# A three-stage transformer layer: prologue joined with cross-attention, grouped attention's end joined with feed-forward

## The chip, the core and the metric

The kernel runs on one core of a Trainium2 chip. The metric is the device time of one execution, in microseconds (us). Engines are named as in the profile: PE (TensorE, matrix products), PEld (its weight loads), DVE (VectorE), ACT (ScalarE), POOL (GpSimd), SP (SyncE, which here only issues DMAs). ACT can issue DMAs too.

## The reference, cut to what matters

```
x   = x + xattn(layernorm(x), ctx)          # x: 8 x 64 x 512, ctx: 8 x 1601 x 512
x   = x + attn(layernorm(x), cache)         # 32 heads, 8 key heads, 16 blocks of 32 cached keys + 64 new ones
x   = x + ffn(layernorm(x))                 # 512 -> 1792 -> 512
xattn: q = (xn @ Wq_d @ W_qk) as 16 heads of 32;  c = ctx @ Wkv_d (1601 x 32)
       out = softmax(q @ c.T / sqrt(32)) @ (c @ Wv_u)
ffn:   W = base + mean(|w - base|) * sign(w - base);  out = (silu(x @ W1.T) * (x @ W3.T)) @ W2.T
```

All in float32. A product that needs the accuracy is made as three products of a high and a low part ("high" a rounded copy, "low" the difference).

## The kernel before, in words

x has 512 tokens: four tiles of 128 rows. Each stage is a block in which every engine has its own program; semaphores order them, and at a block's end all engines meet. There are six blocks.

1. **load_and_constants**: SP loads x (one DMA of 1 MB), the small weights and the contexts of batches 0 and 1 (3.2 MB each). DVE and ACT make the layer norm of all four tiles at once (`normalise`, `root`), PE turns them (L157), ACT copies them out. POOL makes the identity, masks and zeros.
2. **cross_queries**: PE makes the 64 latent query features (L341) and then, head by head, 16 products (L349); for each ACT takes the high part (L358) and DVE the low part (L366) into `q_t`.
3. **cross_attention**: for each batch, `compress` (L580, L584) makes the 32 latent features c of 1601 keys from the context; ACT copies them (L752) and rounds them (L757); POOL makes the low part (L550); SP places them with 15 DMAs (`place_keys`, L497, L499) in the stacked key tile `c_t` (rows: high, low, high). `max_scores` (L618; 16 per batch) with `take_max` on DVE (L813) finds the row maxima, `turn_max` and `shift_row` (L626, L761) put them in `q_t`; then `scores` (L639), exponentials on ACT (L745), values and denominators on PE, pair sums on POOL (L536, L543). Batch b+1's maxima run inside batch b. Beside this, a side job sums |w - base| of the feed-forward weights in 8 slices: SP loads three pieces, POOL subtracts (L529), ACT sums (L766); slice 0 before batch 0, slice b+1 in batch b. The 32 DMAs that gather the selected cache blocks (L293, L296) are the last thing on SP's queue, in batch 6.
4. **rotated_keys**: layer norm 2 and the keys and values of grouped attention.
5. **grouped_attention**: 32 heads in a software pipeline, `head(g, i, this, last, nxt)`: the scores of this head (L1089), turning of the last head's probabilities (L1104, L1105), its mix with the values (L1113 to L1122), queries of the next. After each group of four heads, `output` (L1137) makes the output projection of all four tiles, and DVE adds it to x (L1310). The last head's probabilities are handled by `head(NKV, 0, False, True, False)`, followed by `output` of the last group.
6. **feed_forward**: the three means (L1485, L1428, L1488), layer norm 3, and 14 chunks of 128 hidden features. A chunk's weights are prepared by POOL (difference, L1401), ACT (sign, L1443), DVE (`prepare`: quantise, L1477), ACT (high, L1449) and DVE (low, L1482), two chunks ahead of PE's `gates` (24 products of 512 columns, L1411) and `down` (12 products, L1421).

## Time and profile before

| | |
|---|---|
| three runs, median (lowest, highest) | 978.36 us (976.01, 979.28) |
| the profiled execution's own time | 976.39 us |
| its span, first to last instruction | 974.6 us |
| PE busy | 900.9 us (92%) |
| DVE, ACT, POOL busy | 618.2, 508.8, 402.8 us |
| mean granted TensorE clock | 0.964 of full |

A row of the trace's timeline is: start, duration, engine, line, operation, output<-inputs, shapes, count, and in brackets the idle time of the engine before it with what ended it. Rows with a count are merged.

### The profile page before, as it was taken

Reading aid. Unit: us, or ns where it says so; the run is one execution under the profiler, and the core shown is the slowest. Engines: PE = TensorE matmul, PEld = TensorE weight load, DVE = VectorE, ACT = ScalarE, POOL = GpSimd, SP = SyncE. Lnnn points to the kernel's source line nnn. Section 1 sums busy time; section 2 is a strip of 40 time slices with the busy share of each in tenths; the row PEclk is TensorE's granted clock in tenths of the full one; section 3 lists DMA queues with packets and bytes.
Section 4 is the critical chain, followed back from the end, with each engine's and each line's share of the span. In section 5 each row is a group of like instructions: output and inputs, shape, how many; then the busy total and the mean of one; then the engine's idle time right before and its main releaser. Section 6 shows DMA issues by size and latency. Waiting matters only on the chain. (4 is left out here: it accounts for less than half of the span.)

```text
span 974.6 us, 15256 instructions
## 1 busy us (share of the span) xinstructions
PE 900.9 (92%) x5298; PEld 653.6 (67%) x5298; DVE 618.2 (63%) x994; ACT 508.8 (52%) x995; POOL 402.8 (41%) x264
## 2 busy tenths in 40 slices
PE   4868999999998879999999999999999997599997
PEld 2334455545453658888888888888888886488886
DVE  3453567656671538767577675757757575688883
ACT  2315666666665546636365463645636364355551
POOL 3025778777876024323234232333323231344430
PEclk9857999999999889999999999999999999799999
DMA  9374765642440721111010110101101000465521
GB/s 331 128 257 185 276 258 210 241 157 96 153 143 2 259 76 44 45 33 49 20 51 22 43 43 22 43 22 43 43 22 43 12 1 1 153 206 201 194 90 43
DMA packets 46178, 103.70 MB, mean 106 GB/s; under 512 B 11314, under 2 KB 16434, under 8 KB 45106
## 3 DMA queue, kind: packets, MB, share of 16 engines
q1 hardware_dynamic: 44754, 102.94, 30.8%
q8 instruction: 29, 0.48, 0.2%
q10 hardware_dynamic: 1376, 0.13, 0.2%
q14 instruction: 19, 0.16, 0.0%
HBM read 97.08 MB, written 1.05 MB: 101 GB/s over the span
## 5 line engine op out<-in xcount | busy, mean ns | idle before, releaser
L1336 POOL TENSOR_TENSOR head_probs<-head_probs,inverse_den 128x576 f32<-128x576 f32 x128 | 147.0, 1148 | 298.3 <-DVE inverse_den L1267 298.2
L813 DVE TENSOR_REDUCE max_part<-psum 128x1 f32<-128x804 f32 x128 | 120.9, 989 | 57.7 <-PE psum L618 57.7
L745 ACT ACTIVATE probs<-psum 128x512 f32<-128x512 f32 (+1 forms) x208 | 107.9, 601 | 51.8 <-PE psum L639 47.4
L1214 ACT ACTIVATE head_probs<-psum,neg_max 128x576 f32<-128x576 f32 x128 | 94.6, 739 | 76.6 <-PE psum L1105 43.0
L536 POOL TENSOR_TENSOR prob_sums<-probs 128x1024 f32<-128x1024 f32 x48 | 114.4, 2389 | 26.2 <-PE psum L669 14.0
L1280 DVE TENSOR_REDUCE neg_max<-psum 128x1 f32<-128x576 f32 x128 | 96.1, 754 | 36.2 <-PE psum L1089 28.2
L1260 DVE TENSOR_TENSOR probs_t_low<-psum,probs_t_high 128x512 fp32r<-128x512 f32 x128 | 87.5, 684 | 9.0 <-ACT probs_t_high L1220 7.9
L618 PE MATMUL psum<-c_t,q_t 96*128 96x402 f32 x256 | 80.2, 402 | 11.7 <-DMA c_t<-c_high 7.3
L1089 PE MATMUL psum<-k_high,query_t_high 128*128 (+1 forms) x256 | 84.1, 329 | 5.0 <-DVE query_t_low L1245 2.9
L618 PEld LDWEIGHTS psum<-c_t,q_t 96*128 96x128 f32 x256 | 47.0, 206 | 58.0 <-DVE max_part L813 30.7
L1104 PE MATMUL psum<-ident,head_probs 128*128 128x128 f32 x512 | 78.3, 275 | 5.7 <-DVE mixed_t_low L1305 3.9
L639 PE MATMUL psum<-q_t,c_t 97*128 97x512 f32 (+1 forms) x208 | 73.1, 430 | 6.6 <-ACT probs L745 5.1
L1220 ACT ACTIVATE probs_t_high<-psum 128x512 fp32r<-128x512 f32 x128 | 75.1, 587 | 2.7 <-PE psum L1105 2.7
L1104 PEld LDWEIGHTS psum<-ident,head_probs 128*128 128x128 f32 x512 | 58.0, 140 | 27.4 <-issue 22.1
L1089 PE MATMUL psum<-k_low,query_t_high 128*128 (+1 forms) x256 | 75.5, 295 | 0.0
L1089 PE MATMUL psum<-k_high,query_t_low 128*128 (+1 forms) x256 | 75.3, 294 | 0.0
L1401 POOL TENSOR_TENSOR ffn_quant<-ffn_raw 128x1536 f32<-128x1536 f32 x14 | 49.0, 3500 | 56.4 <-DVE ffn_w_low L1482 52.5
L1310 DVE TENSOR_TENSOR x<-psum,x 128x512 f32<-128x512 f32 x32 | 22.1, 692 | 59.9 <-PE psum L1137 59.9
L652 PE MATMUL psum<-probs,c_nat 128*32 128x512 f32 (+1 forms) x416 | 59.5, 605 | 0.0
L1228 ACT ACTIVATE wo_t_high<-wo_nat 128x512 fp32r<-128x512 f32 x32 | 20.2, 631 | 72.4 <-PE psum L1137 72.4
L529 POOL TENSOR_TENSOR w_raw<-w_raw 128x896 f32<-128x896 f32 x24 | 50.5, 2106 | 16.8 <-DMA w_raw<-in_L_ffn_mean_w_dram 16.8
L639 PEld LDWEIGHTS psum<-q_t,c_t 97*128 97x128 f32 (+1 forms) x208 | 37.9, 189 | 28.7 <-ACT probs L745 21.3
(160 smaller groups left out, 1914.4 us busy)
## 6 DMA issues: line engine op xcount, KB each, us to landing
cache<-in_ctx_dram SPq DMA_DIRECT2D x4, 3202.0 KB, 11.5
ctx_t_odd<-in_ctx_dram SPq DMA_DIRECT2D x4, 3202.0 KB, 11.4
w_raw<-in_L_ffn_w_dram SPq DMA_DIRECT2D x24, 448.0 KB, 5.1
w_raw<-in_L_ffn_mean_w_dram SPq DMA_DIRECT2D x24, 448.0 KB, 6.1
ffn_raw<-in_L_ffn_w_dram SPq DMA_DIRECT2D x42, 256.0 KB, 3.8
ffn_raw<-in_L_ffn_mean_w_dram SPq DMA_DIRECT2D x42, 256.0 KB, 4.1
wq_nat<-in_L_attn_wq_dram SPq DMA_DIRECT2D x32, 256.0 KB, 2.7
wo_nat<-in_L_attn_wo_dram SPq DMA_DIRECT2D x32, 256.0 KB, 2.6
```

Of the source, the lines that this page charges most:

```text
L536: pool.tensor_tensor(sums[u][:, :], prob_buffer(b, 2 * u)[:, :], prob_buffer(b, 2 * u + 1)[:, :], ALU.add).then_inc(s_add, 1)
L618: mm = pe.matmul(psum[:, bank + k, 0:PIECE_KEYS], q_t[0:SHIFT, b, 2 * qt:2 * qt + 2, :].rearrange("p h n -> p (h n)"), c_t[0:SHIFT, b % 3, ...
L639: pe.matmul(psum[0:rows_of(t), n % SCORE_BANKS, :], lhs, rhs[:, half * BANK:(half + 1) * BANK], start=True, stop=True).then_inc(s_sb, 1)
L745: act.activation(prob_buffer(b, t)[0:rows, half * BANK:(half + 1) * BANK], psum[0:rows, n % SCORE_BANKS, :], ACT.Exp, scale=XSCALE).then_i ...
L813: dve.tensor_reduce(max_part[:, qt, pair:pair + 1], psum[:, bank:bank + 2, 0:PIECE_KEYS], AX.XY, ALU.max).then_inc(s_max, 1)
L1089: mm = pe.matmul(psum[:, bank, 0:HALF], q_t[a][:, qt * P:(qt + 1) * P], (k_high, k_low)[b][:, keys], start=(step == 0), stop=(step == 2))
L1104: pe.transpose(bank[:, t * P:(t + 1) * P], probs[:, qt, t * P:(t + 1) * P], core.ident[:, :])
L1214: act.activation(probs[:, qt, :].rearrange("p (a k) -> p a k", a=2), psum[:, 2 * (qt % 2):2 * (qt % 2) + 2, 0:HALF], ACT.Exp, bias=neg_max ...
L1220: act.activation(probs_t[0][:, 0:ST, qt * P:(qt + 1) * P], psum[:, turn_bank(qt), :].rearrange("p (t q) -> p t q", t=ST), ACT.Copy).then_i ...
L1260: dve.tensor_tensor(probs_t[1][:, 0:ST, qt * P:(qt + 1) * P], psum[:, turn_bank(qt), :].rearrange("p (t q) -> p t q", t=ST), probs_t[0][:, ...
L1280: dve.tensor_reduce(neg_max[:, qt:qt + 1], psum[:, 2 * (qt % 2):2 * (qt % 2) + 2, 0:HALF], AX.XY, ALU.max, negate=True).then_inc(s["max"], 1)
L1336: pool.tensor_tensor(probs[:, qt, :], probs[:, qt, :], rden[:, qt:qt + 1].to_broadcast([P, KEYS]), ALU.mult).then_inc(s["norm"], 1)
```

## The change

The first three blocks become one, `cross_attention`, and the last two become one, `attention_and_ffn`.

- **Queries by tile of x.** x is loaded as four DMAs, context 0 as four. Tile 0 is normalised, turned and made into queries at once (`latent_queries(0)`, `queries(0)`), which serves batches 0 and 1. Tiles 1 to 3 come after `compress(0)`: turning, `latent_queries(1)`, and `queries(1)` to `queries(3)` between batch 0's maxima, after the 5th, 8th and 11th. A `queries(j)` is 8 products of 128 columns for head pairs. For tiles 1 to 3 ACT takes the high part of each (two instructions, `queries_high`) and a plain copy (two, `queries_copied`, into the probability buffers, which are still free), and POOL subtracts (two). `scores(0, 0)` waits for all four tiles' low parts.
- **Keys placed from two queues.** For batch 0, SP issues the high and the low rows, ACT the second high rows. For the later batches SP issues high, high, low.
- **The side job** runs one batch later: slice b in batch b, slice 7 in batch 7, its loads behind the cache gather on SP's queue.
- **Early constants.** The three means are made at the start of grouped attention; the exp table is loaded on ACT before batch 0's keys are rounded.
- **Grouped attention's end by tile.** Chunk 0's weights are prepared during the last group of heads (`early_weights`), chunk 1's in the last mix. Feed-forward buffers lie over dead ones (`over`). The last head's turned tiles go to banks 4, 5, 2, 3 and its tail to bank 7 instead of 6. The output projection of the last group is issued in parts, and layer norm 3 runs tile by tile behind them: DVE makes the moments and an offset, ACT the scaled tile (`tile_offset`, `tile_scale`), PE turns it between output parts. The gate products of chunks 0 and 1 are made first for tiles 0 and 1, then for tiles 2 and 3, with 256 columns each.

```diff
+QUERIES_AT = {4: 1, 7: 2, 10: 3}
...
+            pe.wait_ge(s_mask, 1)
+            norm.tile_turn(pe, 0)
+            latent_queries(0)
+            queries(0)
+            pe.wait_ge(s_wkv, 16)
+            compress(0)
+            natural(0)
+            for j in range(1, TT):
+                norm.tile_turn(pe, j)
+            latent_queries(1)
             for i in range(MAXIMA):
                 max_scores(0, i)
+                if i == 1:
+                    compress(1)
+                if i == 3:
+                    natural(1)
+                if i in QUERIES_AT:
+                    queries(QUERIES_AT[i])
             turn_max(0)
+            pe.wait_ge(s_qhi, 2 * TT)
+            pe.wait_ge(s_qlo[1], 2 * (TT - 1))
+            pe.wait_ge(s_wv, 32)
             scores(0, 0)
...
@@ scalar, before batch 0
+            compressed_high(0)
+            act.wait_ge(s_chi, 1)
+            place_part(act, 0, 2 * LKV, c_high)
+            norm.rest_root(act)
...
+            for j in range(1, TT):
+                queries_high(j)
+                queries_copied(j)
...
@@ sync, after place_keys(7)
-            load_pieces(BATCH - 1, 1)
-            load_pieces(BATCH - 1, 2)
+            load_pieces(BATCH - 2, 1)
+            load_pieces(BATCH - 2, 2)
             sp.wait_ge(s_idx, 16)
             gather_cache(core, sp, index)
+            for i in range(3):
+                load_pieces(BATCH - 1, i)
...
@@ tensor, grouped attention: after queries of head 0
+            pe.wait_ge(s_tot, 1)
+            pe.matmul(psum[:, 6, 0:3], ones[:, :], total[:, :], start=True, stop=True).then_inc(s_all, 1)
+            pe.wait_ge(s_co, 1)
             run(pe, head)
+            for qt in range(TT):
+                turn_last(qt)
+            pe.wait_ge(s["wol"], REP * NKV)
+            output_part(0, range(0, 2))
+            mix(NH - 1)
+            output_part(0, range(2, 3))
+            output_part(1, range(0, 3))
+            output_part(0, range(3, 4))
+            output_part(1, range(3, 4))
+            output_part(2, range(REP))
+            norm.tile_turn(pe, 0)
+            output_part(3, range(0, 2))
+            norm.tile_turn(pe, 1)
+            output_part(3, range(2, REP))
+            pe.wait_ge(norm.s_low, TT // 2)
+            gate_products(0, 0, early)
+            norm.tile_turn(pe, 2)
+            gate_products(0, 1, early)
+            norm.tile_turn(pe, 3)
+            for k in range(2):
+                gate_products(1, k, early)
+            pe.wait_ge(norm.s_low, TT)
+            for c in range(2):
+                for k in range(2):
+                    gate_products(c, k, late).then_inc(s_gu[k], 1)
+            down(0)
```

On PE, from the start of the program to batch 0's scores. Before (L341, L349 are the queries, L580 and L584 compress, L618 the maxima):

```order
L157 MATMUL psum<-ident,norm_normed 128x128 x16
L341 MATMUL psum<-xn_t,wq_d 64x512 x4
L349 MATMUL psum<-cq_t,w_qk 64x512 x16
...
L580 MATMUL psum<-ctx_t_odd,wkv_d 32x384 x16
L584 MATMUL psum<-ctx_t_odd,wkv_d 32x65 x16
...
L618 MATMUL psum<-c_t,q_t 128x402 x32
L626 MATMUL psum<-ident,max_row 97x128 x8
```

Now (L752 and L768 are the queries, L635 and L639 compress, L674 the maxima):

```order
L752 MATMUL psum<-xn_t,wq_d 64x384 x4
L674 MATMUL psum<-c_t,q_t 128x402 x4
L635 MATMUL psum<-ctx_t_odd,wkv_d 32x384 x16
L639 MATMUL psum<-ctx_t_odd,wkv_d 32x65 x16
L674 MATMUL psum<-c_t,q_t 128x402 x4
L647 MATMUL psum<-ident,c_parts 128x128 x3
L648 MATMUL psum<-ident,c_parts 65x32
L674 MATMUL psum<-c_t,q_t 128x402 x2
L768 MATMUL psum<-cq_t,w_qk 128x128 x8
L674 MATMUL psum<-c_t,q_t 128x402 x6
L768 MATMUL psum<-cq_t,w_qk 128x128 x8
```

Batch 1's compress and the queries of tiles 1 to 3 have moved from ahead of batch 0's maxima to between them.

On ACT in the same stretch, now (L884 takes the high parts, L891 the copies):

```order
L856 ACTIVATE c_high<-c_parts 128x449
L469 DMA c_t<-c_high 32x384 x4
L471 DMA c_t<-c_high 32x65
L179 ACTIVATE norm_rstd<-norm_rstd 128x3
L225 ACTIVATE xn_t<-psum 128x4x128 x3
L879 ACTIVATE cq_t<-psum 64x384
L910 ACT_TABLE_LOAD
L910 ACTIVATE exp_table_warm<-ones_by_latent 128x1
L851 ACTIVATE c_parts<-psum 128x449
L856 ACTIVATE c_high<-c_parts 128x449
L884 ACTIVATE q_t<-psum 64x16x64 x2
L891 ACTIVATE probs<-psum 32x1024 x2
```

The root of tiles 1 to 3 (L179) stands behind five DMA issues.

On PE at the seam of attention and feed-forward, now (L1403 is the output projection, L215 the turning of a normalised tile, L1413 the gate products):

```order
L1403 MATMUL psum<-wo_t_high,mixed_t_low 128x512
L215 MATMUL psum<-ident,wq_nat 128x128 x4
L1403 MATMUL psum<-wo_t_high,mixed_t_high 128x512
...
L1403 MATMUL psum<-wo_t_high,mixed_t_low 128x512
L1413 MATMUL psum<-attn_x_high,ffn_w_high_4251 128x256 x4
L1413 MATMUL psum<-attn_x_low,ffn_w_high_4251 128x256 x4
L1413 MATMUL psum<-attn_x_high,ffn_w_low_4252 128x256 x4
L215 MATMUL psum<-ident,wq_nat 128x128 x4
L1413 MATMUL psum<-attn_x_high,ffn_w_high_4251 128x256 x4
```

The turning, which stood in one piece of 16 behind all outputs, now lies between output parts and gate products.

## Rows read from the trace of the kernel before

**Rows 1.** The page, part 1: busy time, share and instructions of each engine.
```profile
PE 900.9 (92%) x5298; PEld 653.6 (67%) x5298; DVE 618.2 (63%) x994; ACT 508.8 (52%) x995; POOL 402.8 (41%) x264
```
**Rows 2.** Timeline of PE, from the start to batch 0's scores.
```profile
43.25 2.79 PE L580 MATMUL psum<-ctx_t_odd,wkv_d 128*32 128x384 f32 x32
...
55.17 1.71 PE L618 MATMUL psum<-c_t,q_t 96*128 96x402 f32 x4 [7.29 <-DMA c_t<-c_high]
...
77.32 1.65 PE L639 MATMUL psum<-q_t,c_t 97*128 97x512 f32 x3 [1.11 <-ACT q_t L761]
```
**Rows 3.** Windows: PE, PEld, DVE, ACT, POOL busy, PEclk, DMA share, GB/s.
```profile
10.00:20.00 10.00, 7.20 (x24) 4.29 (x24) 3.18 (x11) 3.00 (x6) 0.00 (x0) 1.00 0.96 412
...
60.00:70.00 10.00, 8.92 (x19) 4.77 (x20) 8.85 (x11) 2.20 (x6) 3.14 (x2) 0.50 0.81 240
```
**Rows 4.** Timelines of SP, DVE, ACT and POOL: unit costs used for the start.
```profile
7.14 0.51 SPq L283 DMA_DIRECT2D cache<-in_ctx_dram  x1
...
44.48 2.52 SPq L497 DMA_DIRECT2D c_t<-c_high  x4
...
63.53 1.89 DVE L813 TENSOR_REDUCE max_part<-psum 128x1 f32<-128x804 f32 x2 [0.23 <-PE psum L618]
...
76.25 1.02 ACT L761 ACTIVATE q_t<-psum 1x1024 fp32r<-1x1024 f32 x1 [12.03 <-PE psum L626]
77.28 1.28 ACT L745 ACT_TABLE_LOAD   x1
...
111.07 1.02 ACT L761 ACTIVATE q_t<-psum 1x1024 fp32r<-1x1024 f32 x1 [0.47 <-PE psum L626]
...
141.42 1.02 ACT L761 ACTIVATE q_t<-psum 1x1024 fp32r<-1x1024 f32 x1 [0.47 <-PE psum L626]
...
310.52 2.35 POOL L543 TENSOR_TENSOR prob_sums<-prob_sums,probs 65x1024 f32<-65x1024 f32 x1
```
**Rows 5.** Timelines of SP and POOL in batches 6 and 7: gather, subtractions, sums.
```profile
287.64 0.37 SPq L296 DMA_DIRECT2D cache<-in_L_attn_v_cache_dram  x1
...
272.64 2.11 POOL L529 TENSOR_TENSOR w_raw<-w_raw 128x896 f32<-128x896 f32 x1
...
293.24 2.37 POOL L536 TENSOR_TENSOR prob_sums<-probs 128x1024 f32<-128x1024 f32 x1 [5.09 <-PE psum L669]
```
**Rows 6.** Timelines of PE and DVE at the start of grouped attention.
```profile
356.51 0.40 PE L1089 MATMUL psum<-k_high,query_t_high 128*128 128x288 f32 x1 [1.41 <-DVE query_t_low L1245]
...
356.37 0.68 DVE L1241 TENSOR_TENSOR wq_t_low<-wq_nat,wq_t_high 128x512 fp32r<-128x512 f32 x1
```
**Rows 7.** Timeline of PE at the seam of attention and feed-forward.
```profile
813.73 1.07 PE L1122 MATMUL psum<-probs_t_low,value_high 128*128 128x512 f32 x4
...
816.30 0.63 PE L1104 MATMUL psum<-ident,head_probs 128*128 128x128 f32 x4 [1.50 <-DVE mixed_t_low L1305]
...
821.41 1.19 PE L1113 MATMUL psum<-probs_t_high,value_high 128*128 128x512 f32 x4 [1.53 <-DVE probs_t_high L1291]
...
841.86 3.68 PE L157 MATMUL psum<-ident,norm_normed 128*128 128x128 f32 x16 [4.15 <-DVE norm_normed L146]
...
850.52 2.04 PE L1411 MATMUL psum<-ffn_x_high,ffn_w_high 128*128 128x512 f32 x4 [4.99 <-DVE ffn_w_low L1482]
```
**Rows 8.** The chain that ended last: start, us, what.
```profile
866.34 5.60 PE psum L1411 x24
871.95 2.76 PE psum L1421 x12
```
**Rows 9.** Timelines of DVE and POOL in the feed-forward chunks.
```profile
851.85 5.22 DVE L1477 SCALAR_TENSOR_TENSOR ffn_quant<-ffn_quant,coeff,ffn_raw 128x512 f32<-128x512 f32 x3 [0.27 <-ACT ffn_quant L1443]
...
869.03 2.06 DVE L1500 TENSOR_TENSOR hidden_low<-hidden,hidden_high 128x512 fp32r<-128x512 f32 x1 [0.70 <-ACT hidden_high L1465]
...
867.03 3.50 POOL L1401 TENSOR_TENSOR ffn_quant<-ffn_raw 128x1536 f32<-128x1536 f32 x1 [4.49 <-DVE ffn_w_low L1482]
...
875.02 3.52 POOL L1401 TENSOR_TENSOR ffn_quant<-ffn_raw 128x1536 f32<-128x1536 f32 x1 [4.49 <-DVE ffn_w_low L1482]
```

More of the change, by code:

```diff
@@ new lines, in gate_products @@
+            def gate_products(c, k, cols):
+                pe.wait_ge(s_wl, 3 * c + k + 1)
+                for step, (a, b) in enumerate(PASSES):
+                    for i in range(DC):
+                        mm = pe.matmul(psum[:, gate_bank(c, k), cols], w_t[c % SLOTS][a][:, k, i * P:(i + 1) * P],
+                                       (xh, xl)[b][:, i, cols], start=(step == 0 and i == 0),
+                                       stop=(step == 2 and i == DC - 1))
+                return mm
@@ new lines, in gates, with down @@
+            def gates(c, k):
+                wait(pe, s_silu if k == 0 else s_h, c - 1)
+                gate_products(c, k, slice(0, TOK)).then_inc(s_gu[k], 1)
+            def down(c):
+                pe.wait_ge(s_hl, c + 1)
+                pe.wait_ge(s_wl, 3 * c + 3)
+                for qt in range(TT):
+                    for step, (a, b) in enumerate(PASSES):
+                        mm = pe.matmul(psum[:, qt, :], hid[c % 2][a][:, qt * P:(qt + 1) * P],
+                                       w_t[c % SLOTS][b][:, 2, :], start=(c == 0 and step == 0),
+                                       stop=(c == CH - 1 and step == 2), skip_group_check=True)
+                mm.then_inc(s_d, 1)
@@ new lines, in _ @@
+            for j in range(TT - 1):
+                norm_tile(j)
+            for j in range(2):
+                norm.tile_low(dve, j)
+            norm_tile(TT - 1)
+            for j in range(2, TT):
+                norm.tile_low(dve, j)
+            for c in range(CH):
+                dve.wait_ge(s_silu, c + 1)
+                dve.wait_ge(s_gu[1], c + 1)
+                wait(dve, s_hl, c)
+                dve.tensor_tensor(hidden[:, :], psum[:, gate_bank(c, 1), :], gate[:, :], ALU.mult).then_inc(s_h, 1)
+                dve.wait_ge(s_hh, c + 1)
+                dve.tensor_tensor(hid[c % 2][1], hidden[:, :], hid[c % 2][0], ALU.subtract).then_inc(s_hl, 1)
+                if c + 2 < CH:
+                    for k in range(3):
+                        quantise(c + 2, k)
+                    for k in range(3):
+                        low(c + 2, k)
@@ L1322, in _ @@
+            dve.wait_ge(s_d, CH)
+            for j in range(TT):
+                dve.tensor_tensor(core.x[:, j, :], psum[:, j, :], core.x[:, j, :], ALU.add).then_inc(s_x, 1)
         @block.gpsimd
```

854 lines of the change are left out of this document (499 added, 355 removed).

## The prediction

> **What bounds the kernel now.** I read the page's engine shares first, then PE's timeline, then the timelines of whatever PE waited for. PE is busy 92% of the span [rows 1], so the change can only win in the stretches where PE idles or runs at half clock. There are two long ones, and the change touches both.
>
> The first is the start. Batch 0's maxima begin at 55.17, after PE has waited 7.29 us for the last placed keys, and its scores begin at 77.32 [rows 2]. Between 60 and 70 PE is busy 8.92 of 10 us, but at a granted clock of 0.50, the 1.2 GHz level [rows 3]: it does one pair of score products per reduction of DVE, every 1.06 us (1.89 / 2 plus 0.23 / 2) [rows 4].
>
> The second is the seam. The last full mix ends at 814.80 (813.73 + 1.07), the gate products begin at 850.52 [rows 7], and from there PE runs without a gap at 8.36 us a chunk (5.60 + 2.76) [rows 8].
>
> **The start.** DMA moves 412 GB/s when loaded [rows 3], so a context (1601 x 512 x 4 bytes, 3.28 MB) takes 8.0 us. SP's small loads end at 7.14 [rows 4], and these are unchanged. Context 0 is thus in at about 17 (7.1 + a latency that I put at 2 + 8), tiles 1 to 3 of x (0.8 MB) at 19, context 1 at 27. Tile 0's queries fit in front of that. compress(0) costs only its last quarter behind the last byte, the two copies 1.1, so the high keys are there at 20.5. Placing five DMAs costs 3.1 us of issue (2.52 for four) [rows 4]. SP issues high and low, 20.5 to 26.8, and with 2 us to land the keys are complete at 29. ACT issues the third part until 23.7. Behind it on ACT is the root of tiles 1 to 3, and behind that the normalised tiles (1.5), turning, copies (1.7) and the latent queries (2.7 at full, 5.4 at half clock): 30 to 33. The queue of ACT, not the keys, releases the first maxima; I take **31.5**.
>
> Then PE has eleven maxima ahead of queries(3), 11 x 1.06 = 11.7, with compress(1) 3.4 (2.79 [rows 2] and its tail), natural(1) 0.8 and three query sets between them. A query set does as many passes as a quarter of the old queries, 1.8 us at full clock. That is 9.6 more if nothing overlaps. PE has half of each 1.06 to spare at full clock, but the waits for banks let it use little of that, and I take off 0.8: 31.5 + 11.7 + 8.8 = 52.0. For the last tile ACT then makes four instructions over 1024 columns, 4 x 1.02 = 4.1, and POOL two, 2 x 2.35 = 4.7 (the nearest row has 65 partitions instead of 32; the duration goes by columns, since 128 partitions take 2.37 [rows 4, 5]). No instruction of this shape is in the trace. Scores at 52.0 + 8.8 = **60.8**, against 77.3: **-16.5**. Compress(1), which would have been late before, is covered by the maxima; what is late next is this chain of copies and subtractions, since scores(0, 0) waits for all of it. Bounds: everything at half clock, 70 (-7); full overlap, 56 (-21).
>
> Batch 0 itself takes 34.8 us from shift row to shift row (76.25 to 111.07), batch 1 30.35 [rows 4]. Of the 4.5 in excess 1.28 is the exp table's load, which moves to where ACT waits anyway; the other 3.2 is mostly half clock. PE will still idle for the subtractions before the scores, so I give back half: **-2.9** (bounds -1.3 and -4.5).
>
> **Batch 7.** The side job's last slice is now in the batch that has no maxima beside it. Its loads stand behind the gather, whose last issue is at 287.64; the first sum starts at 293.24 [rows 5]. With six 0.45 MB loads landing from 293 to 297.5, each of the three subtractions (2.11 [rows 5]) is in POOL's way. POOL is idle a little between sums, so not all 6.3 count; following its queue I get the last sum 3.2 later, and the denominators wait for it: **+3.2** (bounds 0 and +6.3). ACT's three extra sums fit in its waits.
>
> **Start of grouped attention.** The means' matmul waits for DVE behind the second query weight (0.68 [rows 6]) and a 0.16 us scaling; the first scores wait with it: **+0.8** (bounds 0 and +1.5). It was hidden nowhere, since PE already waits 1.41 here.
>
> **The seam.** Between 814.80 and 850.52 lie 35.7 us. PE's work in it: turning four tiles of the last head 2.4 (4 x about 0.6), 14 mix products and 48 outputs at 0.23 (2.76 / 12 [rows 8]) 14.3, the turning of x at most 3.7 [rows 7] and 2.9 at full clock, one matmul 0.35: 19.9. So 15.8 is waiting or slow, and the first eight gate products, at half clock (four take 2.04 [rows 7]), lose 0.23 each, 1.8 more. Now no block ends, and chunks 0 and 1 are prepared. What still waits, following the queues: the mix for the last low tile 1.5, the fourth head's low part 0.6 (ACT has chunk 1's signs in front of it), tile 0's turning 1.0 (DVE has three low parts of chunk 1 in front of its sum, then moments, root on ACT, offset, scaling: 3.1 behind the sum), the low parts of tiles 0 and 1 1.6. That is 4.7. Products of 256 columns instead of 512 cost 0.4 more in total. Sum: 15.8 + 1.8 - 4.7 - 0.4 = **-12.5** (bounds -8, if each norm tile costs a microsecond more, and -15). The chunks' preparation in the last group adds some 4 us of work to DVE and 3 to ACT over three heads; they are busy 63% and 52% [rows 1] and wait for PE at each head's end, so I cost it at nothing (1 us on the mix if that cover is gone). Early buffers, banks and the loop removal cost nothing on any queue.
>
> **Sum.** -16.5 - 2.9 + 3.2 + 0.8 - 12.5 = -27.9. Against the profiled execution's own 976.39 that is 948.5; the median of the three runs is 2.0 higher, and I add half of that: **949.5 us**.
>
> **Rivals.**
> 1. *The query chain at half clock.* PE does compress(1) and the queries at 1.2 GHz, as it did the maxima from 60 to 70 at 89% busy [rows 3]. Scores at 70 instead of 60.8: 959. For: the clock was low there before. Against: then PE had no work between the reductions; compress(1) alone is a run of several us. Chance 0.20.
> 2. *Better than forecast.* Maxima and queries overlap fully and batch 0 runs at full clock: 56 and 1.6 less, 943. Against: the waits for banks. Chance 0.13.
> 3. *The seam pays little.* The tile-by-tile norm is a chain DVE, ACT, DVE, ACT, PE, ACT, DVE, and PE finds too little between: a gain of 6 instead of 12.5, 956. For: four such chains share two queues. Against: 15 output products (3.4 us) stand between tile 0's last one and its turning, and 18 for tile 1. Chance 0.10.
> 4. *Slower, by the preparation of chunks.* DVE and POOL make a chunk every 7.99 us (867.03 to 875.02 [rows 9]), PE needs 8.36. That holds because POOL's 3.5 us subtraction falls on one short DVE instruction, which takes 2.06; where it fell on the three of L1477, they took 5.22 [rows 9] instead of 2.06. The chunks now start in another phase. If POOL stays on L1477, the period is 7.99 + 3.2 = 11.2, and 12 chunks lose 2.8 each: +34, 982. The change turns into a loss above a period of 8.36 + 27.9 / 12 = 10.7. Against: POOL's subtraction waits for the low parts of the chunk before, as it did, so it starts at the same place of DVE's program. Chance 0.02.
>
> The Trainium skill, "SBUF — State Buffer", section "Who interferes with whom", says that a DVE instruction with two SBUF inputs and a GpSimd instruction that reads SBUF exclude each other for a whole instruction, and that issue order decides who waits. The 5.22 and the 2.06 above agree; by that rule alone, with the order left open, rival 4 would be as likely as the forecast, and what sets the order here is the semaphore.
>
> 5. *The change does not do what it says*: SP's loads or a shared bank serialise tile 0's early start, and the start ends where it did. Only the seam is left, less batch 7: 968. Chance 0.03.
>
> **Chances.** Forecast 0.52, rivals as above; the cases join at their edges. A measurement of this kernel can tell about 0.3%, 3 us, from no change. Every case but the fourth lies below 975. With 0.01 for a seam and a start that both disappoint further, and 0.01 for a loss that I don't see: faster 0.96, within 0.3% 0.01, slower 0.03. The range goes from 941 (rival 2 with the better seam) to 961 (rival 1 with 1 us of spread on each side); left out are rivals 4 and 5 and the tails.
>
> **What would show it.** First maxima near 31, with PE's wait ended by the tiles' latent queries; POOL's six subtractions one behind the other, the last ending at the first scores, near 61; shift rows of batch 1 near 92. In batch 7 the last sum 3 us later after the first. First gate products some 22 us behind the last full mix instead of 36, and 8.36 a chunk after them. I am wrong if the wait before the scores is on something else than POOL, if PE's gaps at the seam add up to more than 8 us, or if a chunk takes more than 8.4.

## The result, and the profile after the change

| | before | after |
|---|---|---|
| runs side by side, median (lowest, highest) | 977.18 us (974.94, 979.28) | 946.72 us (943.43, 948.39) |
| ratio, 95% interval | | 0.9684, 0.9645 to 0.9724 |
| the profiled execution's own time, its span | 976.39, 974.6 | 948.39, 946.6 |
| mean granted TensorE clock | 0.964 | 0.976 |

The change takes 30.5 us off the median. The forecast was 949.5.

The page's first part, against [rows 1]: PE has 11 us less busy time in 28 us less span. It does more products (half-width gates), and a smaller share of the span is at half clock (granted 0.976 instead of 0.964).

```profile
PE 889.5 (94%) x5386; PEld 658.9 (70%) x5386; DVE 604.5 (64%) x988; ACT 516.9 (55%) x1005; POOL 416.3 (44%) x270
```

**The start.** Timelines of ACT, PE, POOL and PE, against [rows 2]. The columns are start, duration, engine, line, operation, operands, count, and in brackets the wait with what ended it.

```profile
24.19 0.20 ACT L179 ACTIVATE norm_rstd<-norm_rstd 128x3 f32<-128x3 f32 x1 [4.17 <-issue]
...
28.75 5.38 PE L752 MATMUL psum<-xn_t,wq_d 128*64 128x384 f32 x8 [0.69 <-ACT xn_t L225]
...
34.05 1.28 PE L674 MATMUL psum<-c_t,q_t 96*128 96x402 f32 x4
...
47.11 13.93 POOL L603 TENSOR_TENSOR q_t<-probs,q_t 32x1024 fp32r<-32x1024 f32 x6 [6.17 <-ACT probs L891]
...
61.14 2.24 PE L695 MATMUL psum<-q_t,c_t 97*128 97x512 f32 x4 [2.35 <-POOL q_t L603]
```

ACT takes the roots 4.17 us late, behind its own five DMA issues. The latent queries run at half clock (5.38 for 8 products). The maxima start at 34.05 instead of 55.17. POOL's six subtractions stand one behind the other, 2.32 each, and end at 61.04. PE's wait of 2.35 for them is what releases the scores, 16.2 earlier than at 77.32.

**Batch 7.** Timeline of POOL, against [rows 5]. The first subtraction waits 4.81 us for the load behind the gather, and two more stand between the sums. The last sum ends at 300.44, 29.8 behind the shift row (270.62); before, it was 25.3.

```profile
276.03 2.09 POOL L543 TENSOR_TENSOR w_raw<-w_raw 128x896 f32<-128x896 f32 x1 [4.81 <-DMA w_raw<-in_L_ffn_mean_w_dram]
...
298.07 2.37 POOL L557 TENSOR_TENSOR prob_sums<-prob_sums,probs 65x1024 f32<-65x1024 f32 x1
```

**Start of attention.** PE now waits for the coefficients, 1.97 instead of 1.41 [rows 6].

```profile
344.87 0.40 PE L1309 MATMUL psum<-k_high,query_t_high 128*128 128x288 f32 x1 [1.97 <-DVE coeff L1712]
```

**The seam.** Timeline of PE from the last full mix (804.65 = 803.58 + 1.07) to the first gate product, 20.7 us instead of 35.7 [rows 7].

```profile
803.58 1.07 PE L1342 MATMUL psum<-probs_t_low,value_high 128*128 128x512 f32 x4
...
808.79 1.20 PE L1333 MATMUL psum<-probs_t_high,value_high 128*128 128x512 f32 x4 [0.56 <-DVE probs_t_high L1717]
...
819.29 0.66 PE L215 MATMUL psum<-ident,wq_nat 128*128 128x128 f32 x4 [0.22 <-ACT wq_nat L209]
...
821.70 0.66 PE L215 MATMUL psum<-ident,wq_nat 128*128 128x128 f32 x4 [0.38 <-ACT wq_nat L209]
...
825.33 0.74 PE L1413 MATMUL psum<-attn_x_high,ffn_w_high 128*128 128x256 f32 x4 [1.57 <-DVE attn_x_low L230]
```

The waits add up to 2.7 us. The chain that ended last shows where they come from (start, us, what): chunk 1's transfer ends at 806.38, then POOL's subtraction, ACT's signs and DVE's six instructions for the chunk's weights (with one low part of the last mix between them), and only behind these DVE's sum for tile 0 of x. The last line is one tile's turning.

```profile
801.26 5.12 DMA ffn_raw<-in_L_ffn_mean_w_dram
806.38 0.07 issue
806.44 3.50 POOL ffn_quant L1788
809.96 1.50 ACT ffn_quant L1547
811.49 2.08 DVE ffn_quant L1698 x3
813.57 0.60 DVE mixed_t_low L1727
814.16 1.80 DVE ffn_w_low L1703 x3
815.97 0.61 DVE x L1681
...
827.03 0.44 PE psum L215 x4
```

**The chunks.** The chain again, against [rows 8], and POOL and DVE, against [rows 9]:

```profile
848.88 5.44 PE psum L1413 x24
854.32 2.72 PE psum L1427 x12
```
```profile
841.22 3.50 POOL L1788 TENSOR_TENSOR ffn_quant<-ffn_raw 128x1536 f32<-128x1536 f32 x1 [5.56 <-DVE mixed_t_low L1703]
...
843.28 2.00 DVE L1751 TENSOR_TENSOR probs_t_low<-hidden,probs_t_low 128x512 fp32r<-128x512 f32 x1 [0.70 <-ACT probs_t_low L1592]
```

A chunk takes 8.16 us instead of 8.36, which the prediction did not have. POOL's 3.5 us still fall on the one short instruction of DVE, so rival 4 did not come true.

In sum, between the two profiles: start -16.2, batch 0 -0.7, batch 7 +4.5, start of attention +0.8, heads +1.5, last full mix to the gates of chunk 2 -15.5, twelve chunks -2.4: -28.0, the difference of the spans.

### The profile page after: what moved, and what is told of

Its sections match the earlier page's. It is cut to its first block, busy times and chain, and to the rows that moved or that the text cites. A ratio compares the mean times of both kernels' runs of the same rounds, so it can differ in the third digit from the quotient of the medians.

```text
span 946.6 us, 15443 instructions
## 1 busy us (share of the span) xinstructions
PE 889.5 (94%) x5386; PEld 658.9 (70%) x5386; DVE 604.5 (64%) x988; ACT 516.9 (55%) x1005; POOL 416.3 (44%) x270
## 4 chain that ended last, share of the span: by engine, by line
PE 54%; DVE 5%; ACT 2%; issue 2%; POOL 1%; DMA 1%; DVEq 0%; SPq 0%; ACTq 0%
PE psum L1309 9%; PE psum L1413 8%; PE psum L1357 8%; PE psum L1295 7%; PE psum L1324 6%; PE psum L1427 4%; PE psum L1333 3%; PE psum L1338 3%; PE psum L1342 3%; DVE neg_max L1644 1%; PE psum L1325 1%; PE psum L1334 1%; PE psum L1336 1%; DVE probs_t_low L1624 1%; DVE mixed_t_low L1670 1%
## 5 line engine op out<-in xcount | busy, mean ns | idle before, releaser
L1624 DVE TENSOR_TENSOR probs_t_low<-psum,probs_t_high 128x512 fp32r<-128x512 f32 x124 | 84.8, 684 | 6.4 <-ACT probs_t_high L1525 5.4
L1324 PE MATMUL psum<-ident,head_probs 128*128 128x128 f32 x496 | 75.9, 275 | 3.2 <-DVE mixed_t_low L1670 2.4
L674 PE MATMUL psum<-c_t,q_t 96*128 96x402 f32 x256 | 74.4, 375 | 4.7 <-DVE max_part L945 2.9
L674 PEld LDWEIGHTS psum<-c_t,q_t 96*128 96x128 f32 x256 | 44.1, 192 | 48.1 <-DVE max_part L945 26.5
L1788 POOL TENSOR_TENSOR ffn_quant<-ffn_raw 128x1536 f32<-128x1536 f32 x13 | 45.5, 3506 | 68.0 <-DVE ffn_w_low L1703 26.9
L1525 ACT ACTIVATE probs_t_high<-psum 128x512 fp32r<-128x512 f32 x124 | 72.8, 587 | 0.0
L708 PE MATMUL psum<-probs,c_nat 128*32 128x512 f32 (+1 forms) x416 | 60.4, 613 | 0.0
L1309 PEld LDWEIGHTS psum<-k_high,query_t_high 128*128 128x128 f32 x256 | 48.8, 190 | 9.9 <-ACT head_probs L1519 4.6
L1681 DVE TENSOR_TENSOR x<-psum,x 128x512 f32<-128x512 f32 x32 | 22.1, 690 | 52.4 <-PE psum L1357 52.4
```

The lines of the kernel that those rows point to most:

```text
L674: mm = pe.matmul(psum[:, bank + k, 0:PIECE_KEYS], q_t[0:SHIFT, b, 2 * qt:2 * qt + 2, :].rearrange("p h n -> p (h n)"), c_t[0:SHIFT, b % 3, ...
L1309: mm = pe.matmul(psum[:, bank, 0:HALF], q_t[a][:, qt * P:(qt + 1) * P], (k_high, k_low)[b][:, keys], start=(step == 0), stop=(step == 2))
L1324: pe.transpose(bank[:, t * P:(t + 1) * P], probs[:, qt, t * P:(t + 1) * P], core.ident[:, :])
L1624: dve.tensor_tensor(probs_t[1][:, 0:ST, qt * P:(qt + 1) * P], psum[:, turn_bank(qt), :].rearrange("p (t q) -> p t q", t=ST), probs_t[0][:, ...
```

## The experiments

Each time is a median. Times of one group were measured on one chip beside the same runs of the kernel before, and a ratio is to these. The first group: 1 to 4. The second: 5, 7, 8, 9. The third: 6, 10, 11, 12. The unedited changed kernel ran beside the third group only (0.9701); in the others its ratio of 0.9684 (0.9645 to 0.9724), from another chip, has to serve.

**1. The start alone.** The changed prologue and cross-attention, with grouped attention and feed-forward of the kernel before (whole functions exchanged).

> The prologue and cross-attention of the changed kernel, with the grouped attention and the feed-forward of the kernel before. Theory (the two halves of the change are independent): the first scores stand at 61.1 us and batch 7 gives back about 4.5, so the first product of the heads stands 11.6 us before that of the kernel before (at 344.9), and nothing after it moves: the time is 965 us (977 less 12). A chunk of the feed-forward keeps the 8.36 us of the kernel before. Rival A (the shorter chunk of 8.16 us comes from the start, as from where the program's code or buffers lie): 8.16 a chunk here and 962.5. Rival B (the 1.5 us that the heads lost belongs to the start): first head product at 344.9 but the last full mix only 10 us earlier, 967.

963.88 us, ratio 0.9886 (0.9844 to 0.9929). Scores at 60.7. The first head product stands at 339.9, 5 us earlier than forecast, and the last full mix ends at 798.25, since the heads take 458.4 us. But the end, from there on, takes 164.3 instead of 159.8: the granted clock fell to half in the last head's mix too (its four low products take 1.91 us instead of 1.07). A chunk takes 5.60 + 2.76 = 8.36, so rival A falls, and so does rival B, since the heads lose nothing here.

**2. The seam alone.** The prologue and cross-attention of the kernel before with the joined attention and feed-forward.

> The prologue and cross-attention of the kernel before, with the attention and feed-forward in one block of the changed kernel. Theory: the last full mix ends 1 to 1.5 us later than before (a chunk's weights are prepared by VectorE in the last two heads, and TensorE waits for it), from its end to the gates of chunk 2 it takes 35.9 us where it took 51.4, and 12 chunks at 8.16 instead of 8.36 give 2.4: 977 + 1.2 - 15.5 - 2.4 = 960.5. Rival A (the chunk's length belongs to the start): 8.36 a chunk, 963. Rival B (the seam is gained only because the start made room before it): above 966.

957.82 us, ratio 0.9838 (0.9792 to 0.9883). From the last full mix to the end 141.9 us, as in the changed kernel (141.95), and 8.16 a chunk. The heads take 459.5. The theory's 960.5 was 2.7 too high, and both rivals fall. The ratios of experiments 1 and 2 multiply to 0.9726; the whole change has 0.9684, and 0.9701 (0.9670 to 0.9731) in experiment 12. Within these intervals the halves are independent.

**3. The roots first.**

```diff
+            norm.rest_root(act)
             act.wait_ge(s_chi, 1)
             place_part(act, 0, 2 * LKV, c_high)
-            norm.rest_root(act)
```

> The changed kernel with one step moved: ScalarE takes the roots of tiles 1 to 3 ahead of placing its part of the keys, instead of behind it. Theory (ScalarE's five transfers, 4.1 us, hold up the roots, and with them the tiles' turning, the latent queries and the first maxima, and all up to the scores follows one for one): the roots at 21.4 instead of 24.2, first maxima at 31 instead of 34.05, scores at 58.3 instead of 61.1, 944 against 946.7. Rival A (the keys' placing becomes late by the same step: maxima wait for the keys until about 32.5): scores at 59.6, 945.2. Rival B (TensorE, colder, runs the maxima at half clock for longer and gives it back): scores at 61, 946.7.

944.07 us, ratio 0.9692 (0.9659 to 0.9724). That is the changed kernel's own ratio, so the total does not show what the trace does; experiment 4 beside it took 947.64. The root stands at 21.56 instead of 24.19 (2.6 earlier), the latent queries at 27.37 instead of 28.75 (1.4 earlier), since now the copies of the turned tiles wait behind ACT's issues instead. Maxima at 32.2 (1.8 earlier), POOL's first subtraction at 45.0 instead of 47.1, scores at 59.2, nearer to rival A's numbers than to the theory's, but not by the keys: ACT's 4.2 us of issuing were only shifted to its next instructions.

**4. Tile 3's low part on DVE.**

```diff
-            for j in range(1, TT):            # POOL
+            for j in range(1, TT - 1):
...
+            for odd in range(2):              # DVE, behind negate_max(0)
+                dve.tensor_tensor(query_rows(TT - 1, odd, 2 * LKV, SHIFT), query_bank(TT - 1, odd, LKV),
+                                  query_rows(TT - 1, odd, 0, LKV), ALU.subtract).then_inc(s_qlo[1], 1)
```

> The changed kernel with the low part of query tile 3 taken by VectorE straight from PSUM behind batch 0's maxima (2 x 1.25 us), instead of by ScalarE's copy (2.0 us) and GpSimd (2 x 2.32 us). Theory (GpSimd's six subtractions bound the scores, the shift row is 1.3 us ahead of them): the scores start with the shift row, at 59.9 instead of 61.1, and 945.5 against 946.7. Rival (VectorE's two subtractions end behind the shift row, or its maxima of batch 1 start late for them): scores at 61 or shift row of batch 1 where it was, at 94.15, no change.

947.64 us, the median of five executions; a sixth took 2964 us and is left out. Scores at 65.6, 4.5 later, neither the theory's number nor the rival's. The timeline shows that they did not wait for POOL but for ACT's shift row, and that this was late because two of the three query sets took 3.78 us each, at the 1.2 GHz level, instead of 2.05.

```profile
45.32 3.78 PE L768 MATMUL psum<-cq_t,w_qk 64*128 64x128 f32 x16
...
52.13 3.78 PE L768 MATMUL psum<-cq_t,w_qk 64*128 64x128 f32 x16
...
65.64 2.24 PE L695 MATMUL psum<-q_t,c_t 97*128 97x512 f32 x4 [1.20 <-ACT q_t L860]
```

Experiment 12 shows whether this takes the edit.

**5. Slice 7's first part in the gather.**

```diff
+        if n == at:            # at = 6, in gather_cache
+            between()          # load_pieces(BATCH - 1, 0)
```

> The changed kernel with the first part of slice 7 loaded in the middle of the gather (behind its 7th block, when its buffer has long been free) instead of behind the gather. Theory (batch 7 is lengthened because GpSimd waits 4.8 us for this transfer and then has three subtractions between its sums): GpSimd's first subtraction stands at the end of batch 6's tail (271.2) and ends before the first probabilities; from the shift row to the end of the last sum it takes 25.5 instead of 29.8, as before the change (25.3), and the granted clock in this stretch is 1.00 instead of 0.89; 942.5 against 946.7. Rival (the two other subtractions between the sums are what counts, 2 x 2.1 us, and the clock that TensorE's waiting costs): 28 us and 945.

948.46 us, ratio 0.9734 (0.9700 to 0.9768): no gain, where theory and rival had 942.5 and 945. The DMA's wait is gone (POOL's subtraction stands at 275.67, 0.6 behind the shift row), yet batch 7 takes 27.7 us at a granted clock of 0.88. The theory's 25.5 is wrong and the rival's 28 fits. Of the rival's two causes the clock is what counts here, since in experiment 7 a batch 7 without any subtraction takes 27.7 at 0.88 too.

**6. All keys from SP's queue.**

```diff
-                if b > 0:
-                    place_part(sp, b, 2 * LKV, c_high)
+                place_part(sp, b, 2 * LKV, c_high)
...
-            act.wait_ge(s_chi, 1)
-            place_part(act, 0, 2 * LKV, c_high)
```

> The changed kernel with batch 0's keys placed by SyncE's queue alone (15 transfers in a row), as the kernel before did; ScalarE issues none of them. Theory (ScalarE's five issues cost ScalarE as much as they save SyncE, since the roots and the copies of tiles 1 to 3 stand behind them): the roots at 21.4, the latent queries at 26.0 instead of 28.75, but the last placing is issued at 31 instead of 27 and lands 2 us later: first maxima at 33.3, between the changed kernel's 34.05 and the 32.2 with the roots first; the time within 1 us of the changed kernel's. Rival (the placing from two queues is worth what it saves SyncE, 4 us): first maxima at 36 or later.

945.93 us, against 948.41 of the changed kernel beside it; the ratios are equal (0.9701). The latent queries start at 24.35 and run at full clock (2.79), and now PE waits for the keys:

```profile
24.35 2.79 PE L751 MATMUL psum<-xn_t,wq_d 128*64 128x384 f32 x8 [0.75 <-ACT xn_t L225]
31.11 1.71 PE L673 MATMUL psum<-c_t,q_t 96*128 96x402 f32 x4 [3.97 <-DMA c_t<-c_low]
```

Maxima at 31.1, 3 us earlier than in the changed kernel: the second queue, one of the change's own parts, saves nothing. The last placing is issued at 29.9, not 31, and lands 1.2 later; both had been forecast too late. The clock takes the rest back in this execution: compress(1) behind that wait runs at half clock (4.96 instead of 2.79), and the scores are at 60.8, where two profiles of the changed kernel have 61.1 and 66.0.

The Trainium skill, "Trainium Kernel Development and Optimization", section "Key Constraints", says that DMAs of several issuing engines share the same DMA engines, so that a second one saves issue time only. The runs agree as far as the issue goes: without ACT's help SP has issued its last placing 2.9 us later (29.86 instead of 26.96). They also show what the saving costs, 4.2 us of issuing on ACT, with the roots behind it.

**7. Padding.** The kernel before, with one unused tensor ahead of the feed-forward's buffers.

```diff
     coeff = core.sb("coeff", [P, 3], ctx=own)
+    core.sb("pad_to_64_bytes", [P, 8], ctx=own)
```

> The kernel before with 32 bytes of padding ahead of the feed-forward's quantised chunks, so that these buffers, the split weights and the hidden values begin at a multiple of 64 bytes in each partition (they begin 32 bytes past one in the kernel before; all of these buffers of the changed kernel begin at such a multiple). Nothing else is different. Theory (a 512-column product that reads an operand at 32 past a multiple of 64 takes 0.233 us instead of 0.227): a chunk of the feed-forward takes 8.16 us instead of 8.36, 2.8 us over 14 chunks, ratio 0.997. Rival (the chunk's length has another cause, as the code's place or which transfers run beside it): 8.36 and no change.

The chain of waits of this kernel:

```profile
868.94 5.44 PE psum L1412 x24
874.38 2.72 PE psum L1422 x12
877.10 5.44 PE psum L1412 x24
```

8.16 us a chunk: the padding alone does it, and the theory holds. The split weights began at byte 133088 of a partition, which is 32 past a multiple of 64, and begin at 133120. The high and low parts of x are allocated ahead of the padding and stay where they were. So in the gates only the operand that PE loads as weights moved, and a 512-column product takes 0.227 (5.44 / 24) instead of 0.233 (5.60 / 24). In the down products both operands moved, and they gain half as much (2.72 instead of 2.76 for 12); which of the two counts there was not tried. The total, 971.34 us, ratio 0.9981 (0.9955 to 1.0008), cannot show 2.8 us by itself.

**8. High part of tile 1 first.**

```diff
-                if j > 0:
-                    norm.tile_high(act, j - 1)
+                if j == 1:
+                    norm.tile_high(act, 0)
+                    norm.tile_high(act, 1)
```

> The changed kernel with ScalarE's high part of tile 1 of the feed-forward's input taken ahead of tile 2's root and scaling, instead of behind them. Theory (the first gate products wait 1.57 us for the low part of tile 1, and this for ScalarE's high part, which stands 1.8 us behind its turning): the high part ends at 822.7 instead of 824.5, the low part follows VectorE's of tile 0 and ends at 824.4 instead of 825.3, and the gates start 0.9 us earlier, 0.9 us off the time. Rival (tiles 2 and 3 become late by as much, and the second halves of the gates wait for them): gates 0.9 earlier, the first product on the second half no earlier than now, no change.

946.37 us, ratio 0.9713 (0.9668 to 0.9758). The two low parts now stand together, and PE's wait is 1.02 instead of 1.57:

```profile
821.99 1.28 DVE L230 TENSOR_TENSOR attn_x_low<-psum,attn_x_high 128x512 fp32r<-128x512 f32 x2
```
```profile
823.32 0.74 PE L1413 MATMUL psum<-attn_x_high,ffn_w_high 128*128 128x256 f32 x4 [1.02 <-DVE attn_x_low L230]
```

From the last full mix to the first gate product it still takes 20.6 us (20.7 before the edit). The 0.55 were gained and lost again, because chunk 1's transfer landed 0.5 later behind the last full mix. From POOL's subtraction of chunk 1 to the first gate product it is 18.9 us in the changed kernel and in experiments 2, 3, 4, 5, 6 and 12, whatever stands before, and 18.3 here and in 10 (18.5 in 11). The start of this subtraction behind the last full mix varies from 1.4 us (11) to 3.4 (10), and the first gate product with it, from 20.0 to 21.7. So the seam hangs on this transfer, as far as comparing executions can show it; no run moved the transfer itself.

**9. Whole gates.** The gates of chunks 0 and 1 over 512 columns, behind the fourth tile.

> The changed kernel with the gates of chunks 0 and 1 made over all 512 columns once the four tiles are there, instead of over tiles 0 and 1 first. Theory (the halves of the gates hide the turning and splitting of tiles 2 and 3, and keep TensorE's clock): the first gate product waits until about 829.5, with no work in front but two turnings; 48 products of 0.227 give 10.9, the down products of chunk 0 start at 840.5 instead of 837.8, 2.7 us lost at the full clock and up to 3 more if the granted clock falls in the wait of some 5 us. Rival (the wait moves into the same place anyway, since VectorE's last tile sets the end): less than 1 us lost.

951.86 us, against 946.37 and 948.46 of its neighbours, experiments 8 and 5. From the last full mix to the end it is 148.8 instead of 141.95, 6.85 us more: 5.6 by the later first product, and 1.2 on balance behind it. There the first twelve products ran at the 1.2 GHz level, behind waits of 3.8 and 1.4 us, so that the 48 take 13.7 us instead of 10.9 (48 x 0.227); against this stand 1.6 us for the two turnings and the narrow products that the halves have in this place.

```profile
827.84 0.66 PE L215 MATMUL psum<-ident,wq_nat 128*128 128x128 f32 x4 [3.81 <-ACT wq_nat L209]
829.91 2.08 PE L1413 MATMUL psum<-attn_x_high,ffn_w_high 128*128 128x512 f32 x4 [1.41 <-DVE attn_x_low L230]
831.78 1.91 PE L1413 MATMUL psum<-attn_x_low,ffn_w_high 128*128 128x512 f32 x4
833.49 1.91 PE L1413 MATMUL psum<-attn_x_high,ffn_w_low 128*128 128x512 f32 x4
```

The theory holds, with a little more than its two parts together (2.7 and 3). The halves are worth 6.85 of the 17.9 us between the last full mix and the end.

**10. Edits 3, 5 and 8 together.**

> Three edits together: the roots of tiles 1 to 3 ahead of ScalarE's placing, the first part of slice 7 loaded within the gather, the high part of tile 1 ahead of tile 2's root. Theory (their gains add up: first maxima 1.8 earlier, the DMA's wait of batch 7 gone with up to 2 us, gates 1 us earlier): 943 against 946.7, and 3.5 us less than the changed kernel run beside it. Rival (what is gained in the start and in batch 7 is less than what the place of the clock's fall takes or gives from run to run, 4.5 us in the maxima and 2.4 us in batch 7): a difference under 2 us, of either sign.

943.93 us (six runs, 942.9 to 945.0), ratio 0.9671 (0.9646 to 0.9696), against 948.41 (943.7 to 950.2), ratio 0.9701 (0.9670 to 0.9731) of the changed kernel beside it: 4.5 less in the medians, though the intervals overlap, and two of the six executions of the changed kernel (943.7 and 944.0) are as fast as these. So the theory's 3.5 fits, and the rival's "under 2 us" is not excluded. Here batch 7 kept the full clock and took 26.6 us, 1.3 more than before the change.

**11. The same with PE kept busy in its waits.**

```diff
-                for k in range(2):
+                for k in list(range(2)) * (AGAIN.get(i, 1) if b == 0 else 1):   # {6: 3, 9: 3, 12: 3, 13: 2, 14: 2}
...
+            idle_products(6)
             turn_max(0)
+            idle_products(12)
```

> The three edits, and TensorE is given products whose result is not used, in its waits of the start: batch 0's maxima of tiles 6, 9, 12, 13 and 14 repeated once or twice into the same banks, 6 products of 402 columns ahead of the turning of the maxima and 12 behind it. Theory (the granted clock falls in this stretch because TensorE waits for VectorE and ScalarE again and again): the granted clock stays at 1.00 from the first maxima to the scores, where it was 0.66 to 0.88, and batch 0 starts without its half clock: scores at 58.5 in every run, shift row of batch 1 at 89 (batch 0 takes 30.5 instead of 32.4 to 33), 3 to 5 us less than without. Rival (the clock falls at times that TensorE's work in this stretch does not set): scores and shift row as without, up to 1 us more for the products added.

939.16 us (935.0 to 940.8), ratio 0.9617 (0.9588 to 0.9646), 4.8 less than without, 9.3 less than the changed kernel; its interval lies below that of the changed kernel. Windows: length, busy us of PE, PEld, DVE, ACT and POOL, granted clock, DMA share, GB/s, for the maxima and for batch 0:

```profile
30.92:57.87 26.95, 25.47 (x192) 19.82 (x191) 16.08 (x19) 16.33 (x18) 15.21 (x7) 1.00 0.96 353
57.87:88.00 30.13, 28.56 (x248) 15.37 (x250) 15.98 (x19) 17.82 (x36) 23.89 (x11) 1.00 0.48 174
```

The clock stays at 2.4 GHz through both, the scores are at 57.9, batch 1's shift row at 88.0. The theory holds to within 1 us, and its rival falls.

**12. The changed kernel again.**

> The changed kernel once more, unedited, on the chip and in the rounds of the three others, so that they can be compared with it, and to see what differs between two executions of the same program. Theory (the granted clock falls at another place from one execution to the next, and this is all that differs): first maxima within 1 us of 34, but the scores anywhere from 60.4 to 66; batches 1 to 6 at 176.5; batch 7 between 27.7 and 30; the seam at 142 from the last full mix to the end. Rival (the places are fixed by the program): scores at 61.1 and batch 7 at 29.8, as in its first profile.

948.41 us. The same program, a ratio (0.9701) within the first one's interval, and another profile; the theory holds. The same two windows of this execution and, below, of the first:

```profile
34.69:65.98 31.29, 26.84 (x157) 19.61 (x157) 16.00 (x19) 16.32 (x18) 15.78 (x8) 0.66 0.68 257
65.98:98.41 32.43, 31.19 (x248) 16.89 (x250) 16.01 (x19) 17.93 (x35) 23.21 (x11) 0.90 0.45 162
```
```profile
34.05:61.14 27.09, 20.52 (x157) 14.71 (x157) 15.63 (x19) 16.32 (x18) 15.06 (x7) 0.88 0.80 309
61.14:94.15 33.01, 31.76 (x248) 17.00 (x250) 16.01 (x19) 17.93 (x35) 23.88 (x11) 0.88 0.44 159
```

Scores at 66.0 instead of 61.1, with two query sets at 3.78 us: what experiment 4 showed comes without its edit. In this execution POOL's six subtractions come in pairs with waits between and end at 65.20, and the scores wait for ACT's shift row, which PE's half clock has made late. It is the half clock that bounds the start here.

```profile
53.75 4.68 POOL L603 TENSOR_TENSOR q_t<-probs,q_t 32x1024 fp32r<-32x1024 f32 x2 [1.49 <-ACT probs L891]
60.56 4.64 POOL L603 TENSOR_TENSOR q_t<-probs,q_t 32x1024 fp32r<-32x1024 f32 x2 [2.13 <-ACT probs L891]
```
```profile
65.98 2.25 PE L695 MATMUL psum<-q_t,c_t 97*128 97x512 f32 x4 [1.20 <-ACT q_t L860]
```

**All profiles by stretch** (us; in brackets the granted clock). The columns: first maxima; from there to the scores; batch 0, scores to shift row 1; batch 7, shift row to the last sum's end; from there to the first head product; the heads to the last full mix; from there to the end; span.

| | maxima | to scores | batch 0 | batch 7 | to heads | heads | end | span |
|---|---|---|---|---|---|---|---|---|
| before | 55.2 | 22.1 (0.50) | 33.8 | 25.3 (1.00) | 43.6 | 458.3 | 159.8 | 974.6 |
| 7 | 53.5 | 22.2 (0.50) | 32.9 | 27.7 (0.88) | 42.3 | 458.4 | 161.3 | 974.8 |
| 2 | 54.1 | 22.1 (0.50) | 33.4 | 25.4 (1.00) | 41.7 | 459.5 | 141.9 | 954.5 |
| 1 | 33.9 | 26.8 (0.82) | 32.8 | 28.1 (0.88) | 41.8 | 458.4 | 164.3 | 962.5 |
| after | 34.1 | 27.1 (0.88) | 33.0 | 29.8 (0.89) | 44.4 | 459.8 | 142.0 | 946.6 |
| 12 | 34.7 | 31.3 (0.66) | 32.4 | 27.9 (0.88) | 44.3 | 458.5 | 142.9 | 948.4 |
| 4 | 34.4 | 31.3 (0.66) | 32.4 | 28.8 (0.88) | 41.4 | 459.6 | 142.1 | 946.4 |
| 5 | 34.8 | 31.3 (0.66) | 32.5 | 27.7 (0.88) | 43.0 | 459.9 | 141.9 | 947.7 |
| 8 | 32.2 | 31.2 (0.67) | 32.4 | 27.8 (0.88) | 44.4 | 458.4 | 141.9 | 944.6 |
| 9 | 33.6 | 26.8 (0.82) | 32.8 | 30.1 (0.89) | 44.2 | 459.7 | 148.8 | 952.4 |
| 3 | 32.2 | 27.0 (0.81) | 32.5 | 27.7 (0.88) | 44.4 | 458.3 | 142.5 | 941.1 |
| 6 | 31.1 | 29.7 (0.73) | 32.7 | 28.0 (0.88) | 42.5 | 459.4 | 142.0 | 942.0 |
| 10 | 31.1 | 29.4 (0.71) | 32.7 | 26.6 (1.00) | 44.2 | 459.9 | 143.0 | 943.2 |
| 11 | 30.9 | 26.9 (1.00) | 30.1 | 27.8 (0.94) | 44.4 | 459.8 | 141.2 | 937.7 |

Batches 1 to 6 take 176.4 to 176.5 us in every one. Most of what scatters goes with the granted clock. The 1.5 us of the heads too: they are lost where the clock is at half in the first head, from 345.3 to 348.7 in the first profile of the changed kernel; in executions 3, 8 and 12 it doesn't fall there, and the heads take 458.3 to 458.5, with the chunks' preparation in them. Two columns scatter beside it: the end (141.2 to 143.0 with the new code, experiment 9 left out) at full clock, with the landing of chunk 1's transfer, and batch 7, which takes 27.7 to 30.1 at 0.88 or 0.89.

## Why the prediction was right, and where not

**The total** is 2.8 us below the forecast, well within the range, and the direction was the one given 0.96. The terms fared unevenly, and that the total is so close is in part luck: in the mean the start gave 3 us less than forecast and batch 0 gave 2 less, and the seam with the chunks gave 7 more. "Mean" compares, by the table above, the profiles that hold the old part with those that hold the new one unedited (for the start 3 and 6 of them; for the end experiment 7 is left out, whose chunks the padding shortens); its terms add up to -29.5, near the -30.5 of the medians.

| term | forecast | the two profiles | mean |
|---|---|---|---|
| start, to the scores | -16.5 | -16.2 | -13.4 (76.4, 63.0) |
| batch 0 | -2.9 | -0.7 | -0.7 |
| batch 7 | +3.2 | +4.5 | +2.4 |
| start of attention | +0.8 | +0.8 | +1.0 |
| heads | 0 | +1.5 | +1.0 |
| last full mix to the end | -12.5 | -17.9 | -19.8 |

*The start: the mechanism right, the size right by luck.* Maxima were to begin at 31.5, released by ACT's queue, and began at 34.05, by just that queue; the latent queries took the half-clock price that the text named as its upper bound. Scores at 60.8 by the chain of ACT and POOL, found at 61.14 with PE's wait ended by POOL. POOL's instruction was costed at 2.35 from a row of another width and takes 2.32. But the sum took only tile 3's two subtractions onto the path; the six stand in a row from 47.1 and end 1.2 us behind the shift row (58.82 + 1.02 = 59.84), so that is all that POOL costs here. The row moves with the maxima: in experiment 3 they start 1.8 earlier and it starts 2.1 earlier. And POOL bounds the scores only in an execution whose clock falls late. In 12, 5 and 4 it falls at about 45, within the maxima, and the scores come at 66, half of the way to rival 1, with the wait before them on ACT's shift row. By the prediction's own sign ("the wait before the scores is on something else than POOL") its mechanism fails in 12, an execution of the same program. Rival 1 described the other half of the executions rather than another case (63.3 to 66.1 in 8, 12 and 5, against 60.4 to 61.1 in 9, 1 and the first), and it cost up to 5 us rather than 9, since compress(1) kept its full clock.

*Batch 0: the step that failed is "I give back half".* Nearly all of the half clock stayed (the granted clock of the stretch is 0.87 before and 0.88 now). Experiment 11 gives the size of the whole: with the clock kept, batch 0 takes 30.1 instead of 32.7 in experiment 10. What remains, 0.7, is less than the exp table's 1.28.

*Batch 7: place right, cause mixed.* The prediction had the subtractions in POOL's way and no term for the clock. By experiment 5 the wait for the transfer costs 0 to 2.4 us (27.7 to 30.1 with it, 27.7 without), and by experiments 7 and 5 (27.7 in both, at 0.88) the side job itself nothing there; at full clock it costs 1.3 (26.6 in 10 against 25.3). The other 2.4 is the clock's fall (25.3 and 25.4 against 27.7, all without the side job in this batch). The kernel before can have it as well, in one of three profiles; with the changed batch 7 it is there in ten of eleven.

*Start of attention: right in kind*, 0.56 by the row (1.97 against 1.41). The 0.8 and 1.0 of the table cannot be told from the scatter of this stretch, 41.4 to 44.4 us with the new code. *The preparation of chunks in the heads costs nothing*, as forecast.

*The seam: undersized.* From the last full mix to the gates of chunk 2 the forecast is 3.0 too small. Two of these are waits, forecast at 4.7, that add up to 2.7: the mix for the last low tile waits 0.56 instead of 1.5, the fourth head's low part was in time instead of 0.6, tile 0's turning waits 0.22 instead of 1.0 (and tile 1's 0.38, which was not named), and the low parts 1.57, as forecast. The rest is mostly the turning of x, put at 2.9 for four tiles at full clock; the chain has 0.44 for a tile. No row of the kernel before gave the 0.4 for the narrow products; they cost 0.6 (a 256-column product takes 0.120, and half of a 512-column one is 0.113, 96 times). The old seam was worse than its own profile showed: the clock fell at a second place in two of three executions (1 and 7). And 2.4 us are not the seam's: "8.36 a chunk after them" failed, by the addresses of the buffers. No row of the kernel before shows the cause, though the prediction might have asked why a 512-column product took 0.227 in the output projections and 0.233 in the gates.

*Rival 4 and the skill.* POOL's subtraction was to keep its place by the semaphore, and did: 841.22, across DVE's L1751 (2.00 us) and clear of L1698. The Trainium skill, "SBUF — State Buffer", section "Who interferes with whom", says that issue order decides which of the two waits, and cannot say which order this kernel has. The trace agrees with the exclusion, the 2.00 standing against the same instruction's 0.69 where POOL is idle.

## What to carry to other kernels

In a stretch where PE runs in pieces between waits, cost it at both clock levels and take more than one profile; filling the waits with products that nobody reads bought 4.8 us here, about as much as the three edits of experiment 10 together (4.5). A DMA issue moved to a compute engine's queue is paid by what stands behind it on that engine, so put the short link of the longest chain ahead of it, or leave the issue where it was. When two phases are joined, look for the transfer that the first instructions of the new order wait for: here the seam follows chunk 1's load, and taking tile 1's high part earlier (experiment 8) gained nothing.

## What the runs showed of the hardware

- A 512-column product whose weights began 32 bytes past a multiple of 64 took 0.233 us, and 0.227 at such a multiple, with the other operand and the rest of the program where they were (experiment 7, gates). A chunk takes 2.4% less.
- In the maxima, where PE works in pieces between waits of 0.2 to 0.7 us, the granted clock falls to the 1.2 GHz level, and the point of the fall differed by 12.6 us (42.5 in experiment 8, 55.2 in the first profile) between executions with the same code up to there. With these waits filled it did not fall, nor in the batch behind. The Trainium skill, "TensorE: Matmul & The Clock Gate", section "A second HAM failure mode: psum-queue depth-cycling", tells of a kernel whose clock goes up and down because of many short idle times between groups of products; experiment 11 agrees.
- What one execution lost to the clock in one stretch, another lost elsewhere: the two profiles of the changed kernel differ by 4.8 us at the scores and by 1.8 at the end.
